# Moving the last batch's near scores and three batches' near values from the projection into the second attention

## The chip, the cores and the metric

One core of one Trainium2 chip runs the whole program. The metric is the device time in microseconds of one execution, from three timed runs, and one further execution that was profiled. All times inside the program are taken from that profiled execution and count from the start of its span.

## What is computed

The program is a two-layer language-model tower over 8 sequences (batches) of 512 rows of 256 numbers. Layer 0 is an embedding, a causal attention and a feed-forward block. Layer 1 is the part that matters here. Its attention gives each of 16 heads a window of its own, and scales each head by a gate:

```
windows = [max(4, 256 // 2**h) for h in range(16)]
q, k = split(x @ Wqk + bqk);  v = k
mask = (j <= i) & (j > i - windows[h])
att  = softmax(where(mask, q @ k.T / 4, -inf))
gated = (att @ v) * softmax(x @ Wgate + bgate)[..., None]
out  = gated @ Wproj + bproj
```

Heads 0 to 5 have windows from 256 down to 8 keys; the other ten heads have a window of 4 keys. After it comes a mixture-of-experts block with 8 experts, two for each row, and one shared expert.

## The kernel before

The program is a row of blocks. Inside a block each engine has its own instruction list and waits on semaphores; at the end of a block all engines meet, and the next block begins on all of them together. `project_local` and `attend` are two such blocks, one right after the other, and the change is about them.

**The projection, `project_local`.** It runs over the 8 batches. For each batch TensorE makes queries and keys, VectorE (DVE) adds the bias and writes them to `qkr` (L831), and the six wide heads are turned and split into three bf16 terms: ScalarE (ACT) makes the first and the second (L740, L752), GpSimd (POOL) the third (L789, in `third_term`). SyncE (SP) stores those terms in device memory with six transfers for a batch, three for queries (L643, `q_dram`) and three for keys (L644, `k_dram`), 96 partitions each.

The ten near heads, with 4 keys for each row, are not done on TensorE. SP stores the batch's keys (L627), loads them back shifted by 0, 1, 2 and 3 rows into `near` (L636, a ring of three buffers), and then DVE multiplies keys with queries (L836), sums over 16 elements (L841), adds the mask of the first rows (L846), takes the maximum (L849), subtracts it (L851), waits for ACT's exponential (L744), and makes the shares (L856, L858, L861, L865), which it leaves in `near_shares` (called `pw`, a ring of two). POOL then multiplies shares with keys into `near_values` (called `pv`, L795), adds halves (L800) and adds again into `attn` (L802): this is `near_values(b)`.

DVE's loop has nine turns. Turn n makes the rows of batch n and the near scores of batch n-1, so the ninth turn holds only the near scores of the last batch. POOL's loop for batch b waits (except for the last) until the near product of batch b is done, makes the third term of b, and then does `near_values(b-1)` for b from 1 to 6. The near values of batches 6 and 7 are left to the next block.

**The attention, `attend`.** It handles the six wide heads in 16 units of three heads (two units for each batch). SP loads the unit's terms. TensorE makes scores into a ring of two slots, `psA`; DVE reduces each slot to a row maximum (L1334), and TensorE may fill a slot again only when DVE has reduced it. The maxima are turned, sent to device memory and read back (L1177, L1179) into two further rows of the queries, and a second set of products gives scores from which ACT takes exponentials (L1304). Values and sums come from TensorE (L1262), and DVE divides, multiplies by the gate (L1353) and writes `attn` (L1356). The whole is a software pipeline, four units deep. POOL begins with four memsets (L1128), does `near_values` of batches 6 and 7 (L1118, L1123, L1125), and adds the output bias to the residual (L1134).

Nothing here is planned by costs: the order on each engine is the order of the text.

Of the kernel before, what the change touches and what calls it, by code (L numbers as in the profile page):

```python
# [17 lines left out]
P = 128  # L18
F32 = mybir.dt.float32
# [558 lines left out]
def project_local(nc, res, ident, rstd, shift, w_qk, b_qk, w_g, b_g, q_dram, k_dram, v_dram, k_rows, gates, attn,  # L578
                  near, pv, pw, b_out, bias_out):

# [3 lines left out]
    with ExitStack() as ctx:  # L584
# [10 lines left out]
        zero = k.sb("zero", [B, NW * DW])  # L595
        edge = k.sb("edge", [P, NW])
        prod = k.sb("prod", [P, NW, TG, DW])
# [8 lines left out]
        names = ("raw hi wt tab pad ones edged xn xT xTh xTl q qs vs rows gt gl gexp gdone R h rest m l "  # L606
                 "prod sc0 sc1 sc2 sexp sg sdone pv1 pv2 pv3").split()
        s = {n: k.sem(n) for n in names}
# [6 lines left out]
        def _(sp):  # L615
# [23 lines left out]
            def terms(b):  # L639
                par = b % 2  # L640
                sp.wait_ge(s["l"], b + 1)
                for term in range(NTERM):
                    sp.dma_start(q_dram[b, :, DK * term:DK * (term + 1), :], part[0:PW, par, term, 0, :]).then_inc(s_out[par], 16)  # L643
                    sp.dma_start(k_dram[b, :, DK * (2 - term):DK * (3 - term), :], part[0:PW, par, term, 1, :]).then_inc(s_out[par], 16)  # L644

            for b in range(B):
                rows(b)
                if b >= 1:
                    terms(b - 1)
            terms(B - 1)  # L650
            for n in range(2):
                sp.wait_ge(s_out[n], 16 * NL * (B // 2))
                sp.wait_ge(s_vout[n], 16 * (B // 2))
# [57 lines left out]
        def _(act):  # L711
# [49 lines left out]
            for b in range(B):  # L761
# [8 lines left out]
                if b + 2 < B:  # L770
                    normed(b + 2)
            near_exp(B - 1)

        @block.gpsimd
        def _(pool):
# [15 lines left out]
            def near_values(b):  # L791
                pool.wait_ge(s["sdone"], 3 * b + 3)
                if b >= 1:
                    pool.wait_ge(s["pv3"], b)
                pool.tensor_tensor(pv[:].rearrange("p n t (h d) -> p (n t h) d", d=DK),  # L795
                                   near[:, b % 3].rearrange("p n t (h d) -> p (n t h) d", d=DK),
                                   pw[:, b % 2].rearrange("p n t h -> p (n t h)").unsqueeze(2).to_broadcast([P, NW * TG * DH, DK]),
                                   ALU.mult).then_inc(s["pv1"], 1)
# [11 lines left out]
            pool.wait_ge(s["pv3"], B - 2)  # L810
            pool.wait_ge(s["l"], B)

        @block.vector
        def _(dve):
# [39 lines left out]
            def near_shares(b):  # L854
# [7 lines left out]
                dve.wait_ge(s["sg"], b + 1)  # L862
                if b >= 2:
                    dve.wait_ge(s["pv1"], b - 1)
                dve.tensor_tensor(pw[:, b % 2], sc, ssum[:].unsqueeze(1).to_broadcast([P, NW, TG, DH]), ALU.mult  # L865
                                  ).then_inc(s["sdone"], 1)
# [29 lines left out]
            dve.wait_ge(s["edged"], 2)  # L896
            for n in range(B + 1):
                if n < B:
                    rows(n, (0, 1))
                if n >= 1:  # L900
                    near_products(n - 1)
                if n < B:
                    rows(n, (2, 3))
# [6 lines left out]
                if n < B:  # L910
                    gate_logits(n)
                    rests(n)
                if n >= 1:
                    near_shares(n - 1)
                if n < B:
                    gate_shares(n)
            dve.wait_ge(s["sdone"], 3 * B)

# [154 lines left out]

def attend(nc, tag, windows, bands, q_dram, k_dram, v_dram, m_dram, gates, near, pv, pw, ident, attn, res, bias):

# [14 lines left out]
    with ExitStack() as ctx:  # L1090
# [14 lines left out]
        s_load, s_values = ([k.sem(f"{name}{n}") for n in range(2)] for name in ("load", "values"))  # L1105
        names = "const scoresA max topT_ps topT m_out m_in scoresB exp pv outT turned rec norm near1 near2 near3 biased".split()
        s = {n: k.sem(n) for n in names}
# [6 lines left out]
        def _(pool):  # L1114
            def near_values(n, b):
                if n:
                    pool.wait_ge(s["near3"], n)
                pool.tensor_tensor(pv[:].rearrange("p n t (h d) -> p (n t h) d", d=DK),  # L1118
                                   near[:, b % 3].rearrange("p n t (h d) -> p (n t h) d", d=DK),
                                   pw[:, b % 2].rearrange("p n t h -> p (n t h)").unsqueeze(2).to_broadcast([P, NW * TG * DH, DK]),  # L1120
                                   ALU.mult).then_inc(s["near1"], 1)
# [7 lines left out]
            pool.wait_ge(s["const"], 4)  # L1129
            for n in range(2):  # L1130
                near_values(n, B - 2 + n)
# [4 lines left out]
            pool.wait_ge(s["near3"], 2)  # L1136

# [149 lines left out]
        def _(act):  # L1287
            def stage(u):
                for what, n in events(windows, u):
# [24 lines left out]
        def _(dve):  # L1314
            def stage(u):
                for what, n in events(windows, u):
# [27 lines left out]
                    elif what == "OUT":  # L1344
# [6 lines left out]
                        if windows is not None:  # L1351
# [1667 lines left out]
def tower(nc, a):  # L3019
    Kit.used.clear()  # L3020
    with ExitStack() as ctx:
# [16 lines left out]
        with ExitStack() as ctx1:  # L3038
# [11 lines left out]
            with nc.sbuf_tensor("attn1", [P, NT, D], F32) as attn, nc.sbuf_tensor("gates", [P, NT, H], F32) as gates, \  # L3050
                    nc.sbuf_tensor("bias_out", [P, D], F32) as bias_out:
                with nc.sbuf_tensor("near", [P, 3, NW, TG, DW], F32) as near, \
                        nc.sbuf_tensor("near_values", [P, NW, TG, DW], F32) as pv, \
                        nc.sbuf_tensor("near_shares", [P, 2, NW, TG, DH], F32) as pw:
                    project_local(nc, res, ident, rstd1, shift1, a["w_qk1"], a["bqk"], a["w_g1"], a["bgate"], q1_dram, k1_dram, v1_dram,
                                  k_rows, gates, attn, near, pv, pw, a["bproj"], bias_out)
                    attend(nc, "att1", windows, bands, q1_dram, k1_dram, v1_dram, m_dram, gates, near, pv, pw, ident, attn,
                           res, bias_out)
# [59 lines left out]
```

## Time and profile before

| | us |
|---|---|
| median of 3 timed runs | 1414.05 |
| lowest, highest | 1412.55, 1414.31 |
| profiled execution, whole | 1406.67 |
| its span | 1404.9 |
| PE (TensorE) busy in the span | 1228.1 |
| DVE busy | 838.8 |
| POOL busy | 682.2 |
| ACT busy | 646.5 |

The span is the profiled execution without what lies around it (1.77 us). The projection runs from some 517 us to 655.70 us, the second attention from there to some 793 us. Busy shares of the whole say little about these two stages; the rows below are read from the boundary between them.

### The profile page before, as it was taken

The page shows a single profiled execution, that of the slowest core. Times are in us where ns is not written, and L with a number is a line of the kernel's source. Part 1 is how long each engine was busy: PE and PEld are TensorE (multiplying, and loading weights), DVE is VectorE, ACT ScalarE, POOL GpSimd, SP SyncE. Part 2 cuts the span into 40 slices and gives each one's busy share as a digit, 9 for nine tenths or more (in the row PEclk, how much of TensorE's full clock was granted, in tenths as well). Part 3 has the DMA queues.
Part 4 walks back from the last instruction along what each step waited for, and adds up shares of the span by engine and source line. Part 5 has one row for each costly group of instructions (what it writes and reads, how often), then busy time and mean ns, then how long its engine had stood idle before and what let it go on. Part 6 is the DMA issues. An engine that isn't in the chain of part 4 may idle for free. (4 is left out here: it accounts for less than half of the span.)

```text
span 1404.9 us, 29240 instructions
## 1 busy us (share of the span) xinstructions
PE 1228.1 (87%) x9665; PEld 961.1 (68%) x9666; DVE 838.8 (60%) x1784; ACT 646.5 (46%) x1249; POOL 682.2 (49%) x621
## 2 busy tenths in 40 slices
PE   5886999999978949892899785989989999999996
PEld 3664555555546837771666674989977888888885
DVE  4998788888837957995655394633333333333332
ACT  2882566666665544440344463222323334333332
POOL 6856687777352220877800000366224555555453
PEclk9996899999999977775899998999999999999999
DMA  2497999999500004665354321000347335465331
GB/s 56 141 280 230 273 278 280 276 288 292 130 3 2 1 28 133 190 185 153 93 115 97 105 80 41 16 26 28 108 162 216 54 52 141 114 166 139 52 56 21
DMA packets 123608, 179.16 MB, mean 128 GB/s; under 512 B 26953, under 2 KB 84592, under 8 KB 123512
## 3 DMA queue, kind: packets, MB, share of 16 engines
q1 hardware_dynamic: 106808, 159.62, 39.2%
q0 software_dynamic: 16704, 18.31, 7.9%
q8 instruction: 54, 0.88, 0.3%
q14 instruction: 42, 0.34, 0.1%
HBM read 104.60 MB, written 74.18 MB: 127 GB/s over the span
## 5 line engine op out<-in xcount | busy, mean ns | idle before, releaser
L1637 DVE TENSOR_REDUCE att_top<-att_psS 128x4 f32<-128x512 f32 (+2 forms) x192 | 194.9, 1037 | 41.6 <-PE att_psS L1524 40.0
L2851 POOL DMA_INDIRECT out<-ffn1c_y,ffn_table x71 | 112.3, 1582 | 164.3 <-DMA out<-ffn1c_y,ffn_table 76.7
L2984 DVE TENSOR_TENSOR ffn1c_hid<-ffn1c_psG,ffn1c_sil 128x512 f32<-128x512 f32 x71 | 49.1, 692 | 135.7 <-PE ffn1c_psG L2889 135.7
L1608 ACT ACTIVATE att_prob<-att_psS 128x1024 f32<-128x1024 f32 (+1 forms) x96 | 83.3, 887 | 61.6 <-PE att_psS L1538 61.6
L1518 PE MATMUL att_psS<-pairs_ka,pairs_qa 48*128 48x384 f32 (+3 forms) x512 | 100.3, 401 | 9.8 <-DMA pairs_ka<-k_parts 5.3
L2889 PE MATMUL ffn1c_psG<-ffn_high,ffn1c_xh 128*128 x284 | 96.4, 421 | 4.8 <-DVE ffn1c_xl L2975 2.7
L1608 ACT ACTIVATE pairs_part<-att_psS 128x1024 f32<-128x1024 f32 (+1 forms) x96 | 83.0, 888 | 34.3 <-PE att_psS L1538 34.3
L2593 POOL DMA_INDIRECT ffn_rows<-normed_rows,ffn_table x71 | 70.0, 986 | 55.4 <-DVE ffn_gate L2467 25.4
L2444 POOL DMA_INDIRECT slots<-ffn1b_entry,ffn1b_sloti x64 | 64.1, 1002 | 61.1 <-DVE ffn1b_sloti L2532 23.8
L1538 PE MATMUL att_psS<-pairs_qa,pairs_ka 50*128 50x256 f32 (+3 forms) x512 | 88.8, 388 | 3.0 <-DVE att_top L1637 0.9
L2889 PE MATMUL ffn1c_psG<-ffn_high,ffn1c_xl 128*128 x284 | 89.9, 397 | 0.0
L2889 PE MATMUL ffn1c_psG<-ffn_low,ffn1c_xh 128*128 x284 | 89.6, 397 | 0.0
L2949 ACT CAST ffn1c_hh<-ffn1c_psH 128x512 fp32r<-128x512 f32 x71 | 41.7, 587 | 87.2 <-PE ffn1c_psH L2900 85.9
L1334 DVE TENSOR_REDUCE att_top<-att_psA 128x2 f32<-128x768 f32 (+3 forms) x64 | 51.3, 813 | 47.7 <-PE att_psA L1215 46.9
L1524 PE MATMUL att_psS<-m_later,m_half 64*128 64x128 bf16 x1024 | 77.9, 234 | 0.0
L2942 ACT ACTIVATE ffn1c_sil<-ffn1c_psG 128x512 f32<-128x512 f32 x71 | 42.5, 598 | 64.9 <-PE ffn1c_psG L2889 64.9
L2975 DVE TENSOR_TENSOR ffn1c_xl<-ffn1c_psX,ffn1c_xh 128x256 fp32r<-128x256 f32 x71 | 30.2, 425 | 69.9 <-ACT ffn1c_xh L2935 67.9
L1304 ACT ACTIVATE att_prob<-att_psB 128x384 f32<-128x384 f32 (+4 forms) x112 | 48.9, 472 | 49.0 <-PE att_psB L1229 48.5
L1518 PEld LDWEIGHTS att_psS<-pairs_ka,pairs_qa 48*128 48x128 f32 x512 | 53.3, 201 | 26.2 <-issue 14.6
L2699 ACT ACTIVATE ffn1b_sil<-ffn1b_psG 128x256 f32<-128x256 f32 x64 | 24.6, 385 | 101.0 <-PE ffn1b_psG L2660 79.5
L1538 PEld LDWEIGHTS att_psS<-pairs_qa,pairs_ka 50*128 50x128 f32 x512 | 43.6, 188 | 34.7 <-issue 23.1
L2957 ACT ACTIVATE ffn1c_y<-ffn1c_psY,ffn_gate 128x256 f32<-128x256 f32 x71 | 33.7, 474 | 68.4 <-PE ffn1c_psY L2914 61.6
(397 smaller groups left out, 3534.9 us busy)
## 6 DMA issues: line engine op xcount, KB each, us to landing
prep_raw<-in_w_all SPq DMA_DIRECT2D x27, 512.0 KB, 5.7
experts_hi<-ffn0w_room SPq DMA_DIRECT2D x27, 512.0 KB, 6.4
experts_lo<-prep_lo SPq DMA_DIRECT2D x27, 512.0 KB, 7.4
ffn_high<-experts_hi SPq DMA_DIRECT2D x24, 512.0 KB
ffn_low<-experts_lo SPq DMA_DIRECT2D x24, 512.0 KB
near<-near_keys SPq DMA_DIRECT2D x32, 320.0 KB
q_parts<-pairs_part SPq DMA_DIRECT2D x8, 1024.0 KB
k_parts<-pairs_part SPq DMA_DIRECT2D x16, 512.0 KB
```

Of the source, the lines that this page charges most:

```text
L1304: act.activation(dst, src, ACT.Exp, scale=0.25).then_inc(s["exp"], 1)
L1334: dve.tensor_reduce(dst, src, AX.X, ALU.max).then_inc(s["max"], 1)
L1518: pe.matmul(psS[:, bank, g, col:col + cols], qa[r, u % LOADED, q, P * i:P * (i + 1)], ka[r, u % LOADED, q, 0:cols], start=True, stop=True, ...
L1524: mm = pe.matmul(psS[:, bank, g, col + cols - P:col + cols], half[r, part, :], later[r, part, :], start=False, stop=True, tile_position=(6 ...
L1538: mm = pe.matmul(psS[:, bank, g, col:col + cols], ka[r, v % LOADED, q, P * j:P * (j + 1)], qa[r, v % LOADED, q, P * j:S], start=True, stop ...
L1608: act.activation(dst, src, ACT.Exp, scale=0.25).then_inc(s["exp"], 1)
L1637: dve.tensor_reduce(dst, src, AX.X, ALU.max).then_inc(s["max"], 1)
L2444: pool.indirect_dma_start(out=self.dram["table"], in_=self.entry[:, t, n, :], in_offset=None, out_offset=bass.IndirectOffsetOnAxis(ap=self ...
L2593: pool.indirect_dma_start(out=rows[:, t % 4, :], out_offset=None, in_=dram["rows"], in_offset=bass.IndirectOffsetOnAxis(ap=table[:, t:t + ...
L2851: pool.indirect_dma_start(out=rows_out, in_=y[:, t.buf, :], in_offset=None, out_offset=bass.IndirectOffsetOnAxis(ap=table[:, t.value:t.val ...
L2889: mm = pe.matmul(psG[:, t.par, g, :], x[:, t.par, P * c:P * (c + 1)], w[:, bass.ds(at, 1), col:col + F1], start=(q == 0), stop=(q == 5))
L2984: dve.tensor_tensor(hid[:, t.par, :], psG[:, t.par, 1, :], sil[:, t.par, :], ALU.mult).then_inc(s["act"], 1)
```

## The change

DVE's loop now has eight turns, so that the last batch's near scores leave the projection. A new class `Late` holds what they need in SBUF: the last batch's near queries (copied there by POOL at the end of the projection), the mask of the first rows, the scores, maximum, sums and shares. `attend` begins on DVE with `late_shares`, the nine instructions of those scores, ahead of the first maximum of unit 0; ACT does their exponential ahead of its walk. `near_values` of three batches (5, 6, 7) now run on POOL in `attend`; the first must wait until DVE has read the products out of `pv`, which both use. `near_shares` has three buffers instead of two. In the projection, POOL makes the third term of batches 6 and 7 without waiting for a near product. The last batch's three stores of keys' terms are issued by ACT's queue, the three of queries still by SP's. SP waits for the last `near` loads before the block ends.

```
 project_local, SP, terms(b):
-        sp.dma_start(k_dram[b, ...], part[0:PW, par, term, 1, :]).then_inc(s_out[par], 16)
+        if b < B - 1:
+            sp.dma_start(k_dram[b, ...], part[0:PW, par, term, 1, :]).then_inc(s_out[par], 16)
+ at its end: sp.wait_ge(s_near[(B - 1) % 3], 16 * NW * ((B - 1) // 3 + 1))
 project_local, ACT, after the loop:
-        near_exp(B - 1)
+        act.wait_ge(s["l"], B)
+        for term in range(NTERM):
+            act.dma_start(k_dram[B - 1, :, DK * (2 - term):DK * (3 - term), :], part[0:PW, (B - 1) % 2, term, 1, :])
 project_local, POOL:
         for b in range(B):
-            if b < B - 1:
+            if b < B - 2:
                 pool.wait_ge(s["prod"], b + 1)
             third_term(b)
-            if 1 <= b < B - 1:
+            if 1 <= b < B - 2:
                 near_values(b - 1)
+        pool.wait_ge(s["qs"], TG * B)
+        pool.tensor_copy(late.q_rows[:], qkr[:, (B - 1) % 2, :, PW:D]).then_inc(s["kept"], 1)
 project_local, DVE:
-        for n in range(B + 1):        # near scores of n - 1 in every turn n >= 1
+        for n in range(B):
 attend, POOL:
     def near_values(n, b):
+        pool.wait_ge(s["late"], 9 if b == B - 1 else 2)
-    for n in range(2): near_values(n, B - 2 + n)
+    for n in range(3): near_values(n, B - 3 + n)
 attend, ACT:
+        act.wait_ge(s["late"], 5)
+        act.activation(late.scores[:], late.scores[:], ACT.Exp, scale=0.25).then_inc(s["late_exp"], 1)
         walk(act, stage, groups)
 attend, DVE:
+        def late_shares():            # each waits for the one before it, the sums also for ACT
+            pv = near[:, b % 3] * late.q_rows           # 128x2560, late = 1
+            sc = reduce add over 16 of pv               # 128x160, late = 2
+            sc[:, :, 0, :] += late.edge                 # 128x40
+            late.largest = reduce max of sc             # 128x40
+            sc -= late.largest                          # 128x160, late = 5
+            late.sums = reduce add of sc                # after late_exp
+            late.shares = reciprocal of late.sums
+            late.shares *= gates of the last batch      # 128x40
+            pw[:, b % 3] = sc * late.shares             # 128x160, late = 9
+        late_shares()
         walk(dve, stage, groups)
```

The lines inside `late_shares` are written short here. All its operands are in SBUF; in the projection the scores were in PSUM.

## Rows read from the trace of the kernel before

**Rows 1.** Windows of the second attention: us, busy by engine, clock, DMA share, GB/s.
```profile
core 0: us, PE busy (x) PEld busy (x) DVE busy (x) ACT busy (x) POOL busy (x), PEclk, DMA share, GB/s
663.00:671.00 8.00, 6.92 (x54) 5.15 (x52) 5.82 (x10) 0.00 (x0) 7.76 (x4) 0.67 0.62 110
703.00:711.00 8.00, 7.33 (x91) 5.42 (x88) 4.90 (x11) 3.88 (x9) 0.00 (x0) 1.00 0.48 104
```

**Rows 2.** Timeline, PE and DVE as the attention starts: start, duration, instruction, idle before.
```profile
660.57 0.40 PE L1212 MATMUL att_psA<-bands_never,bands_idb 128*128 128x256 bf16 x1 [25.71 <-DMA att_ka<-k_parts]
...
662.76 0.50 PE L1213 MATMUL att_psA<-bands_mask_q,bands_idb 128*128 128x384 bf16 x1 [0.41 <-DVE att_top L1334]
...
661.75 1.42 DVE L1334 TENSOR_REDUCE att_top<-att_psA 128x2 f32<-128x768 f32 x2 [10.45 <-PE att_psA L1215]
```

**Rows 3.** Timeline of SP's queue at the end of the projection.
```profile
637.72 0.76 SPq L643 DMA_DIRECT2D q_parts<-qkv_part  x1
...
641.71 0.74 SPq L644 DMA_DIRECT2D k_parts<-qkv_part  x1
647.76 0.74 SPq L643 DMA_DIRECT2D q_parts<-qkv_part  x1
...
651.71 0.74 SPq L644 DMA_DIRECT2D k_parts<-qkv_part  x1
```

**Rows 4.** Waits of SP's queue, 600 to 700 us: total, times, longest.
```profile
SPq L652 <- DMA k_parts<-qkv_part: 2.4, 1, 2.4
```

**Rows 5.** Timeline of ACT: the last batch's second term.
```profile
638.50 1.05 ACT L752 CAST qkv_part<-qkv_rest 96x1024 bf16<-96x1024 f32 x1 [0.91 <-DVE qkv_rest L889]
```

**Rows 6.** Timeline of POOL, from the projection's end into the attention.
```profile
631.87 2.13 POOL L789 TENSOR_TENSOR qkv_part<-qkv_rest,qkv_part 96x1024 bf16<-96x1024 f32 x1 [2.76 <-DVE qkv_prod L836]
...
643.03 4.70 POOL L789 TENSOR_TENSOR qkv_part<-qkv_rest,qkv_part 96x1024 bf16<-96x1024 f32 x1
655.70 5.33 POOL L1128 MEMSET att_ka<- 2x1536 bf16 x4 [7.97 <-POOLq L584]
661.11 4.55 POOL L1118 TENSOR_TENSOR near_values<-near,near_shares 128x2560 f32<-128x2560 f32 x1
665.74 2.88 POOL L1123 TENSOR_TENSOR near_values<-near_values 128x1280 f32<-128x1280 f32 x1
668.70 1.54 POOL L1125 TENSOR_TENSOR attn<-near_values 128x640 f32<-128x640 f32 x1
```

**Rows 7.** Windows of one us at the two ends of term stores, columns as Rows 1.
```profile
643.00:644.00 1.00, 0.00 (x0) 0.00 (x0) 1.00 (x1) 0.00 (x0) 1.00 (x2) 0.50 0.41 144
645.00:646.00 1.00, 0.00 (x0) 0.00 (x0) 0.97 (x2) 0.00 (x0) 1.00 (x1) 0.50 0.23 80
654.00:655.00 1.00, 0.00 (x0) 0.00 (x0) 0.00 (x0) 0.00 (x0) 0.00 (x0) 0.50 0.12 42
```

**Rows 8.** Timeline of DVE: the last batch's near scores, first to last.
```profile
642.63 3.12 DVE L836 TENSOR_TENSOR qkv_prod<-near,qkv_qkr 128x2560 f32<-128x2560 f32 x1 [2.29 <-DMA near<-near_keys]
645.79 2.83 DVE L841 TENSOR_REDUCE qkv_psS<-qkv_prod 128x160 f32<-128x2560 f32 x1
648.65 0.21 DVE L846 TENSOR_TENSOR qkv_psS<-qkv_psS,qkv_edge 128x40 f32<-128x40 f32 x1
...
649.25 0.33 DVE L851 TENSOR_TENSOR qkv_psS<-qkv_psS,qkv_smax 128x160 f32<-128x160 f32 x1
...
650.75 0.20 DVE L861 TENSOR_TENSOR qkv_ssum<-qkv_psS,gates 128x40 f32<-128x40 f32 x1
650.98 0.32 DVE L865 TENSOR_TENSOR near_shares<-qkv_psS,qkv_ssum 128x160 f32<-128x160 f32 x1
```

**Rows 9.** Line L1353: count, then duration in ns, min/median/max, first and last start.
```profile
L1353 DVE TENSOR_TENSOR att_rec<-att_rec,gates x16: 170/172/1947, 687.5 to 792.3; 128x12 f32<-128x12 f32 x16
```

**Rows 10.** Timeline of DVE and of POOL: its slowest execution, and what POOL ran.
```profile
693.70 1.95 DVE L1353 TENSOR_TENSOR att_rec<-att_rec,gates 128x12 f32<-128x12 f32 x1 [0.28 <-DVE att_rec L1349]
...
679.40 18.53 POOL L1134 TENSOR_TENSOR m_res<-m_res,bias_out 128x1024 f32<-128x1024 f32 x8
```

**Rows 11.** Line L836: duration in ns, min/median/max.
```profile
L836 DVE TENSOR_TENSOR qkv_prod<-near,qkv_qkr x8: 2815/2830/3157, 544.8 to 642.6; 128x2560 f32<-128x2560 f32 x8
```

More of the change, by code:

```diff
@@ L578, in project_local @@
 def project_local(nc, res, ident, rstd, shift, w_qk, b_qk, w_g, b_g, q_dram, k_dram, v_dram, k_rows, gates, attn,
-                  near, pv, pw, b_out, bias_out):
+                  near, pv, pw, late, b_out, bias_out):
     with ExitStack() as ctx:
@@ L595, in project_local @@
         zero = k.sb("zero", [B, NW * DW])
-        edge = k.sb("edge", [P, NW])
+        edge = late.edge
         prod = k.sb("prod", [P, NW, TG, DW])
@@ L650, in _ @@
             terms(B - 1)
+            sp.wait_ge(s_near[(B - 1) % 3], 16 * NW * ((B - 1) // 3 + 1))
             for n in range(2):
@@ L771, in _ @@
                     normed(b + 2)
-            near_exp(B - 1)
+            act.wait_ge(s["l"], B)
+            for term in range(NTERM):
+                act.dma_start(k_dram[B - 1, :, DK * (2 - term):DK * (3 - term), :], part[0:PW, (B - 1) % 2, term, 1, :]
+                              ).then_inc(s_out[(B - 1) % 2], 16)
         @block.gpsimd
@@ L909, in _, with __init__ @@
                     near_scores(n - 1)
-                if n < B:
-                    gate_logits(n)
-                    rests(n)
+                gate_logits(n)
+                rests(n)
                 if n >= 1:
                     near_shares(n - 1)
-                if n < B:
-                    gate_shares(n)
-            dve.wait_ge(s["sdone"], 3 * B)
+                gate_shares(n)
+            dve.wait_ge(s["sdone"], 3 * (B - 1))
+            dve.wait_ge(s["gdone"], 3 * B)
+class Late:
+    def __init__(self, k):
+        self.q_rows = k.sb("q_rows", [P, TG, DW])
+        self.edge = k.sb("edge", [P, NW])
+        self.scores = k.sb("scores", [P, NW, TG, DH])
+        self.largest, self.sums, self.shares = (k.sb(n, [P, TG, DH]) for n in ("largest", "sums", "shares"))
 class Unit:
@@ L1071, in make, with attend @@
         pool.wait_ge(s_done, n + 4 * len(self.windows))
-def attend(nc, tag, windows, bands, q_dram, k_dram, v_dram, m_dram, gates, near, pv, pw, ident, attn, res, bias):
+def attend(nc, tag, windows, bands, q_dram, k_dram, v_dram, m_dram, gates, near, pv, pw, late, ident, attn, res, bias):
     groups, HG = (len(windows), len(windows[0])) if windows else (NHG, H // NHG)
@@ L1105, in attend @@
         s_load, s_values = ([k.sem(f"{name}{n}") for n in range(2)] for name in ("load", "values"))
-        names = "const scoresA max topT_ps topT m_out m_in scoresB exp pv outT turned rec norm near1 near2 near3 biased".split()
+        names = "const scoresA max topT_ps topT m_out m_in scoresB exp pv outT turned rec norm late late_exp near1 near2 near3 biased".split()
         s = {n: k.sem(n) for n in names}
@@ L1129, in _ @@
             pool.wait_ge(s["const"], 4)
-            for n in range(2):
-                near_values(n, B - 2 + n)
+            for n in range(3):
+                near_values(n, B - 3 + n)
             for b in range(B):
@@ L1314, in _ @@
         def _(dve):
+            def late_shares():
+                b, sc = B - 1, late.scores
+                dve.tensor_tensor(pv[:], near[:, b % 3], late.q_rows[:].unsqueeze(1).to_broadcast([P, NW, TG, DW]),
+                                  ALU.mult).then_inc(s["late"], 1)
+                dve.wait_ge(s["late"], 1)
+                dve.tensor_reduce(sc[:].rearrange("p n t h -> p (n t h)"),
+                                  pv[:].rearrange("p n t (h d) -> p (n t h) d", d=DK), AX.X, ALU.add).then_inc(s["late"], 1)
+                dve.wait_ge(s["late"], 2)
+                dve.tensor_tensor(sc[:, :, 0, :], sc[:, :, 0, :], late.edge[:].unsqueeze(2).to_broadcast([P, NW, DH]), ALU.add
+                                  ).then_inc(s["late"], 1)
+                dve.wait_ge(s["late"], 3)
+                dve.tensor_reduce(late.largest[:], sc[:].rearrange("p n t h -> p t h n"), AX.X, ALU.max).then_inc(s["late"], 1)
+                dve.wait_ge(s["late"], 4)
+                dve.tensor_tensor(sc[:], sc[:], late.largest[:].unsqueeze(1).to_broadcast([P, NW, TG, DH]), ALU.subtract
+                                  ).then_inc(s["late"], 1)
+                dve.wait_ge(s["late_exp"], 1)
+                dve.tensor_reduce(late.sums[:], sc[:].rearrange("p n t h -> p t h n"), AX.X, ALU.add).then_inc(s["late"], 1)
+                dve.wait_ge(s["late"], 6)
+                dve.reciprocal(late.shares[:], late.sums[:]).then_inc(s["late"], 1)
+                dve.wait_ge(s["late"], 7)
+                dve.tensor_tensor(late.shares[:], late.shares[:], gates[:, tiles_of(b), PH:H], ALU.mult).then_inc(s["late"], 1)
+                dve.wait_ge(s["late"], 8)
+                dve.tensor_tensor(pw[:, b % 3], sc[:], late.shares[:].unsqueeze(1).to_broadcast([P, NW, TG, DH]), ALU.mult
+                                  ).then_inc(s["late"], 1)
             def stage(u):
```

32 lines of the change are left out of this document (16 added, 16 removed).

## The prediction

> **What bounds the kernel now.** The change touches one place, the boundary at 655.70 us between the projection and the second attention, so I read the windows first, to see what the attention is bound by, and then the timelines of each engine around the boundary.
>
> In the attention's steady part TensorE is busy 7.33 of 8 us and DVE 4.90 [rows 1]. TensorE sets its pace, but only once the pipeline runs. At its start the two work in turns: TensorE fills two slots, and the third slot waits for DVE's first maximum (0.41 us of idle before the matmul at 662.76) [rows 2]. A microsecond lost at the start, by TensorE or by DVE, is a microsecond of the whole, since the stage after it begins only when the attention has ended.
>
> TensorE has nothing to do for 25.71 us before its first matmul of the attention at 660.57, and what ends this is a load of key terms [rows 2]. Followed back: the loads start with the block at 655.70, where POOL's first memset also starts [rows 6]; the block starts when SP has seen the last stored term land, a wait of 2.4 us [rows 4] after the sixth issue, which began at 651.71 and ended at 652.45 [rows 3]; the first of the six began at 647.76, when POOL's third term of the last batch was done (643.03 + 4.70 = 647.73) [rows 3, 6]. That instruction has two reasons to be late. ACT had its input ready at 639.55 (638.50 + 1.05) [rows 5], but POOL was in `near_values` until 643.03; and it then took 4.70 us where the one for the batch before took 2.13 [rows 6], because DVE's near product ran from 642.63 to 645.75 [rows 8]: 645.75 plus some 2 us is its end. DVE's own chain for the last batch ends at 651.30 [rows 8], 3.1 us before the last stored byte, so it does not set the end of the block.
>
> **The change part by part.** I call the start of the attention block T0; it is 655.70 now.
>
> *The third term.* The last batch's no longer queues behind `near_values(5)`, and DVE's near product of batch 7 is gone. It starts at 639.6 and, at 2.13 us, ends at 641.75: 6.0 us earlier than 647.73. That of batch 6 loses its wait, but DVE's product of batch 6 runs then and holds it to the same place, so I price it at nothing (631.87 + 2.13 still).
>
> *The stores.* SP is busy with batch 6's six stores until 642.45 (641.71 + 0.74) [rows 3]. Three more issues, at (651.71 - 647.76) / 5 = 0.79 us each, bring it to 644.8, and with the 2.4 us of landing [rows 4] and the 0.85 us from there to T0 (655.70 - 652.45 - 2.4) the block would start at 648.1, 7.6 us earlier. ACT's three issues run beside SP's, from 641.8 to 644.2, if they cost what SP's cost. But the data must also get through. Batch 6's stores are still being drained until 645.56: in that stretch the DMA share is 0.41 and the rate 144 GB/s, and it falls to 0.23 in the microsecond from 645 [rows 7]. The share never rises above this 0.41 while only term stores are in flight, though six were queued, so I take it as the rate at which these stores drain, from whichever queue they come. The last batch's six stores hold 6 x 98,304 bytes, which at 144 GB/s is 4.1 us after 645.56, so 649.65. Now the data end at 654.3 (share 0.12 of some 0.39 in the microsecond from 654) [rows 7]. So T0 moves by 4.65 us, to 651.05. The two ends are 4.65 (the stores of both queues share one drain) and 7.6 (only the issues count). I take 4.65, nearest to the measured drain.
>
> The Trainium skill has a rule on this (DMA: Bandwidth & Descriptors, "Issuing engines are not separate DMA queues"): transfers started by different engines run on the same 16 DMA engines, and starting them from several saves only the sequencer's time. By this rule the gain is the 4.65, and by a queue of its own for ACT the 7.6. The trace has no ACT store to compare.
>
> *POOL's copy of the queries* (128x640) lies after the third term and before 645; a 128x640 addition takes 1.54 us [rows 6], which is covered by the stores. SP's new wait for the near loads is over at 642.63 [rows 8]. Both cost nothing unless the stores end before 643.3.
>
> *DVE's nine instructions in the attention.* In the projection they took from 642.63 to 651.30, 8.67 us with ACT's exponential among them [rows 8]. Now they begin at T0. Without any stall DVE would be free at T0 + 8.7, while its first maximum now starts at T0 + 6.05 (661.75 - 655.70) [rows 2]. That alone costs 2.6 us, and it is the low end.
>
> But there is a stall. L1353 multiplies two small SBUF operands and takes 0.172 us in the median of 16 and 1.947 at most [rows 9]. The slow one started at 693.70 and ended at 695.65; POOL was then in a row of eight additions from 679.40, 2.316 us each, the seventh of which ended at 695.61 [rows 10]. So a DVE instruction with two SBUF inputs waits until the POOL instruction that was there first is over, and POOL waits the same way (the 4.70 us above). Of the nine, five have two SBUF inputs: the product, the mask, the subtraction, the gate, and the last. In the projection all but the product read their scores from PSUM.
>
> The Trainium skill says the same (SBUF — State Buffer, "Who interferes with whom"): the shared port pair is an exclusive lock, and a DVE instruction with two SBUF inputs contends with a GpSimd instruction that reads SBUF, not with one that only writes. By it the four memsets at the block's start do not hold up the product, nor it them; no row here shows that pair.
>
> Laid out from T0, each number with its row: product 2.83 (the median of L836) [rows 11], sum 2.83, to 5.7 with gaps. This releases POOL's first `near_values`; its memsets were over at 5.33 [rows 6]. The mask (0.21) starts first, since an instruction behind its own engine's semaphore begins some 0.04 us later and another engine's some 0.08 (645.79 after 645.75, and 631.87 after 631.79). Ends 5.93. POOL's product of 4.55 then runs to 10.48, and the subtraction waits for it: 10.81. POOL's addition of 2.88, queued meanwhile, runs to 13.69. The exponential, sum and reciprocal fall in this. The gate multiplication waits: 13.89. POOL's second addition of 1.54 runs to 15.43, and the last instruction waits for it: 15.76 [rows 6, 8]. The first maximum starts at T0 + 15.8 and not at T0 + 6.05: **9.75 us later**. TensorE has then filled two slots and waits with the third. If DVE's last instruction slips in ahead of POOL's second addition, it is 8.2.
>
> *The clock.* TensorE was granted 0.50 (1.2 GHz) while idle before the attention [rows 7], and 0.67 as a mean of the stretch 663 to 671, after which it runs at 1.00 [rows 1]. With a second idle stretch of some 10 us right after its first two slots, it is at the lower level again for work that now has some of the higher. I put 0.5 us on it, an estimate between 0 and 1.5.
>
> *POOL* has 8.97 us more (4.55 + 2.88 + 1.54) and starts later; its bias additions end near T0 + 52 of a stage of 137 us: hidden, and as many L1353 meet them as now.
>
> **The sum.** -4.65 + 9.75 + 0.5 = +5.6 us on the profiled execution's 1406.67, so 1412.3. The timed median stands 7.4 above that execution; the same addition to it gives 1414.05 + 5.6 = **1419.6 us**.
>
> **The rivals.**
>
> *A. No lock at the wrong moment (not slower).* If POOL's memsets wait for DVE's first product, they end at T0 + 2.83 + 5.33 = 8.16, and POOL's first product comes when DVE has only its last small instruction left. The place is the first 8 us of the attention, and it decides at whether the memsets end before DVE's sum does. Price 2.6 instead of 9.75 + 0.5, so -4.65 + 2.6 = -2.0: 1412.0. For it: POOL's L789 did wait for a DVE product. Against it: that one reads SBUF, a memset does not. With the stores at their other bound it would be -5.0, 1409.
>
> *B. ACT's queue drains beside SP's.* T0 moves by 7.6, and with the stall the sum is -7.6 + 10.25 = +2.65: 1416.7. For it: the trace shows one queue only. Against it: 0.41 of the DMA engines looks like a limit of the transfers' form.
>
> *C. POOL gets in first.* If POOL's product goes ahead of the mask, the mask ends at 10.5, the subtraction waits for POOL's 2.88 (13.7), the gate for its 1.54 (15.5), and the last for the next batch's 4.55: T0 + 20.3, a delay of 14.3, so +10.1: 1424.2. For it: both are released by the same event. Against it: the 0.04 us.
>
> **How the numbers follow.** Forecast 0.6, A 0.17, B 0.13, C 0.10. Only a difference above 0.2%, 2.8 us, can be told from none. Of the forecast's own 1416 to 1422 nearly all is slower by more than this (0.54); C adds 0.10 and B, which lies on the line, 0.05: slower 0.69. A is split between faster (0.09) and the same (0.08), B gives 0.07 and the forecast 0.05 to the same; 0.02 of the latter I move to faster for what I don't see: same 0.20, faster 0.11. The range takes in A's centre at its low end and C at its high end: 1411.5 to 1425.
>
> **What would show it.** The third term of the last batch starts at 639.6 and takes 2.1 us. The attention's loads start near 651. In the attention's first 16 us the subtraction, the gate multiplication and the last of `late_shares` show durations of 4.5, 2 and 1.8 us instead of 0.2 to 0.3, each ending with a POOL instruction, and TensorE idles some 10 us before its third slot, ended by L1334's successor. If those instructions are short, the forecast is wrong and A holds; if the loads start near 648, B does.

## The result, and the profile after

The changed kernel takes 1417.07 us in the median of 16 runs (1414.43 to 1423.14), beside 1413.68 of the kernel before (16 runs, 1402.65 to 1417.38). The ratio is 1.0041, with a 95% interval of 1.0023 to 1.0060: slower by 0.41%, or 5.8 us of 1413.68 (the two medians by themselves are 3.4 us apart, the two means 5.5). The forecast was 5.6 us slower, and 1419.6 us as a time.

The profiled execution of the changed kernel has a span of 1416.5 us, 11.6 more than the one before. Only 5.8 of these belong to the change. ACT's second term of the last batch, the last mark ahead of what the change moves, starts at 644.98 where it started at 638.50 [rows 5]. These 6.48 us are not the change's: SP's first issue of the projection comes 7.31 us later (524.95, 517.64 before), so they were lost ahead of it, in instructions that the change leaves alone, and 0.83 came back in the projection's first batches. Both are within the spread of the runs. The interval from the same mark of batch 6 to this one is 13.00 us, and 12.98 before. So the stretches below are counted from that mark, from the block's start T0 (where POOL's first memset starts), and to the end of DVE's last output of the attention (792.87 before, 805.17 after):

| | before | after | difference |
|---|---|---|---|
| from the mark to T0 | 17.20 | 13.58 | -3.62 |
| from T0 to DVE's first maximum | 6.05 | 15.09 | +9.04 |
| from T0 to the attention's end | 137.17 | 146.61 | +9.44 |
| from the mark to the attention's end | 154.37 | 160.19 | +5.82 |
| from there to the end of the span | 612.03 | 611.33 | -0.70 |

The start of the attention on DVE, with the columns of the timelines before: start, duration, instruction, idle before it. The first nine are the near scores that stood in the projection [rows 8].

```profile
658.60 2.83 DVE L1335 TENSOR_TENSOR near_values<-near,late_q_rows 128x2560 f32<-128x2560 f32 x1 [11.78 <-PEq L584]
661.46 2.82 DVE L1338 TENSOR_REDUCE late_scores<-near_values 128x160 f32<-128x2560 f32 x1
664.32 0.20 DVE L1341 TENSOR_TENSOR late_scores<-late_scores,late_edge 128x40 f32<-128x40 f32 x1
664.55 0.42 DVE L1344 TENSOR_REDUCE late_largest<-late_scores 128x40 f32<-128x160 f32 x1
665.01 4.15 DVE L1346 TENSOR_TENSOR late_scores<-late_scores,late_largest 128x160 f32<-128x160 f32 x1
669.56 0.43 DVE L1349 TENSOR_REDUCE late_sums<-late_scores 128x40 f32<-128x160 f32 x1 [0.40 <-ACT late_scores L1328]
670.02 0.40 DVE L1351 RECIPROCAL late_shares<-late_sums 128x40 f32<-128x40 f32 x1
670.46 1.54 DVE L1353 TENSOR_TENSOR late_shares<-late_shares,gates 128x40 f32<-128x40 f32 x1
672.03 1.70 DVE L1355 TENSOR_TENSOR near_shares<-late_scores,late_shares 128x160 f32<-128x160 f32 x1
673.65 1.41 DVE L1377 TENSOR_REDUCE att_top<-att_psA 128x2 f32<-128x768 f32 x2
```

POOL in the same stretch, and its third term of the last batch ahead of it [rows 6]:

```profile
646.11 2.12 POOL L794 TENSOR_TENSOR qkv_part<-qkv_rest,qkv_part 96x1024 bf16<-96x1024 f32 x1 [5.84 <-ACT qkv_part L754]
648.17 0.71 POOL L816 COPY late_q_rows<-qkv_qkr 128x640 f32<-128x640 f32 x1
658.56 5.33 POOL L1144 MEMSET att_ka<- 2x1536 bf16 x4 [9.68 <-POOLq L584]
664.43 4.55 POOL L1134 TENSOR_TENSOR near_values<-near,near_shares 128x2560 f32<-128x2560 f32 x1 [0.54 <-DVE late_scores L1338]
669.06 2.88 POOL L1139 TENSOR_TENSOR near_values<-near_values 128x1280 f32<-128x1280 f32 x1
672.02 1.53 POOL L1141 TENSOR_TENSOR attn<-near_values 128x640 f32<-128x640 f32 x1
```

Read the two together. All three DVE instructions that wait have two SBUF inputs. The subtraction (L1346, 0.33 us in the projection) starts at 665.01 and ends at 669.16; POOL's product ends at 668.98. The gate multiplication (0.20 before) ends at 672.00, POOL's addition at 671.94. The last (0.32 before) ends at 673.73, POOL's second addition at 673.55. The reductions between them run side by side with POOL unharmed, and so do the memsets and DVE's product: 5.33 and 2.83 us, both as long as alone. The Trainium skill's exception (SBUF — State Buffer, "Who interferes with whom": a GpSimd instruction that only writes SBUF does not contend) agrees with these two rows.

TensorE's third slot, by its timeline, waits for DVE; the idle time was 0.41 us [rows 2]:

```profile
663.53 0.40 PE L1228 MATMUL att_psA<-bands_never,bands_idb 128*128 128x256 bf16 x1 [22.47 <-DMA att_ka<-k_parts]
...
674.66 0.50 PE L1229 MATMUL att_psA<-bands_mask_q,bands_idb 128*128 128x384 bf16 x1 [9.34 <-DVE att_top L1377]
```

The stores, by the queues' timelines of ACT and SP and by windows of one us (columns as Rows 1):

```profile
648.25 2.94 ACTq L776 DMA_DIRECT2D k_parts<-qkv_part  x3
649.42 2.50 SPq L643 DMA_DIRECT2D q_parts<-qkv_part  x3
```

```profile
649.00:650.00 1.00, 0.00 (x0) 0.00 (x0) 0.00 (x0) 0.00 (x0) 0.00 (x0) 0.50 0.41 145
655.00:656.00 1.00, 0.00 (x0) 0.00 (x0) 0.00 (x0) 0.00 (x0) 0.00 (x0) 0.50 0.35 123
657.00:658.00 1.00, 0.00 (x0) 0.00 (x0) 0.00 (x0) 0.00 (x0) 0.00 (x0) 0.50 0.04 15
```

SP's last wait of the projection, 2.4 us before [rows 4], with what it waits for (us in total, times, longest):

```profile
SPq L654 <- DMA q_parts<-qkv_part: 6.1, 1, 6.1
```

The last issue is over at 651.92, and the data still flow until 657. What ends the block is the drain, as in the forecast, and not the issues.

### The profile page after: what moved, and what is told of

It reads as the page before. It is cut to its first block and busy times, and to the rows that moved or that the text cites. A ratio compares the mean times of both kernels' runs of the same rounds, so it can differ in the third digit from the quotient of the medians.

```text
span 1416.5 us, 29239 instructions
## 1 busy us (share of the span) xinstructions
PE 1230.6 (87%) x9665; PEld 963.9 (68%) x9666; DVE 845.2 (60%) x1784; ACT 646.8 (46%) x1249; POOL 682.7 (48%) x622
```

## The experiments

Each kernel was timed in turns with the kernel before; its ratio to it and the interval stand with it. Its trace is counted from the same mark. The whole of a run scatters by several us, so the stretches carry the verdicts, but they scatter too: where the attention's code is the same or nearly so, its stage differs by 0.5 us (136.92 to 137.45 in the five kernels without the nine in it), by 0.57 (138.95 and 139.52) and by 1.40 (146.61 and 145.21), and the stretch from the mark to T0 by up to 1.3. A difference below some 1.5 us between two single traces is therefore not read as an effect. The table sums up what follows (us).

| kernel | mark to T0 | T0 to first maximum | T0 to end | mark to end |
|---|---|---|---|---|
| before | 17.20 | 6.05 | 137.17 | 154.37 |
| changed | 13.58 | 15.09 | 146.61 | 160.19 |
| POOL waits for all nine | 12.66 | 8.54 | 138.95 | 151.61 |
| without the nine | 12.92 | 6.24 | 137.45 | 150.37 |
| changed, SP stores all | 12.13 | 15.09 | 145.21 | 157.34 |
| near values of 5 moved, ACT stores | 12.87 | 6.21 | 137.20 | 150.07 |
| before, ACT stores | 17.01 | 6.44 | 136.92 | 153.93 |
| near values of 5 moved, SP stores | 13.59 | 6.04 | 137.06 | 150.65 |
| changed, POOL's work in pieces | 12.88 | 11.03 | 141.88 | 154.76 |
| POOL waits, SP stores all | 11.80 | 8.54 | 139.52 | 151.32 |
| the nine spread | 13.06 | 6.38 | 141.28 | 154.34 |
| the nine spread, POOL in pieces | 12.90 | 6.50 | 136.85 | 149.75 |

### POOL waits for all nine

```
 attend, POOL, near_values:
-        pool.wait_ge(s["late"], 9 if b == B - 1 else 2)
+        pool.wait_ge(s["late"], 9)
```

> The changed kernel, but POOL starts the first near values of the attention only when all nine near-score instructions of DVE are done, so that no POOL instruction that reads SBUF runs beside them. Theory (lock): in the changed kernel the nine take 15.1 us because three of them wait out a POOL instruction; here they take 8.7 us, as in the projection before, no one of the small ones over 0.5 us, DVE's first maximum starts 8.7 us into the attention instead of 15.1, and the stage that took 146.6 us takes about 140. On the whole about 6.4 us less than the changed kernel, 1 us less than the kernel before. Rival (the nine are slow by themselves in SBUF, or are slowed by the key loads that run beside them): they take 15 us again and nothing moves.

The nine take 8.59 us (658.19 to 666.78), from its timeline of DVE:

```profile
664.60 0.32 DVE L1346 TENSOR_TENSOR late_scores<-late_scores,late_largest 128x160 f32<-128x160 f32 x1
...
666.22 0.20 DVE L1353 TENSOR_TENSOR late_shares<-late_shares,gates 128x40 f32<-128x40 f32 x1
666.45 0.33 DVE L1355 TENSOR_TENSOR near_shares<-late_scores,late_shares 128x160 f32<-128x160 f32 x1
666.69 1.42 DVE L1377 TENSOR_REDUCE att_top<-att_psA 128x2 f32<-128x768 f32 x2
```

The same instructions in the same place, with the same key loads beside them, are back at 0.32, 0.20 and 0.33. One changed constant gives back 7.66 us of the stage (146.61 to 138.95; the expectation was about 140). The ratio is 0.9964 (0.9932 to 0.9997). The lock is shown, the rival is out.

### Without the nine

```
 attend, DVE:    -        late_shares()
 attend, ACT:    -        act.wait_ge(s["late"], 5) and the exponential
 attend, POOL:   -        pool.wait_ge(s["late"], ...)
```

> The changed kernel without the last batch's near scores: the nine DVE instructions, ACT's exponential and POOL's waits for them are left out, so the last batch's near values are made from old shares. This shows the gain at the boundary alone. Theory: the attention stage is back at 137.2 us (before: 137.2, changed: 146.6) and its start stays where the changed kernel has it, 3.6 us earlier than before when counted from the last batch's second term; so about 9.4 us less than the changed kernel and 3.6 less than before. Rival (part of the longer stage comes from POOL's third near value or from the clock): the stage stays 1 us or more above 137.2.

The stage is back at 137.45, with POOL's third near value in it. So this third near value costs nothing that can be seen, and the nine and their stall are all but 0.3 of the 9.44 us. Ratio 0.9952 (0.9915 to 0.9989).

### All stores on SP

```
 project_local, SP:   -  if b < B - 1:      (the three key stores of every batch)
 project_local, ACT:  -  its three stores
```

> The changed kernel, but all six stores of the last batch's terms are issued by SP, none by ACT. Theory (the stores drain at some 143 GB/s whichever queue they come from): the attention starts within 0.5 us of where the changed kernel has it, 13.6 us after the start of the last batch's second term, and the time is unchanged. Rival (the issues set the end): three issues more on SP's queue at 0.79 us each make the start 2.4 us later.

T0 comes 1.45 us earlier than in the changed kernel, not 2.4 later. So the rival is out, but the expectation (within 0.5 us) missed too. SP's last issue ends at 652.46, and its wait behind it is 2.9 us, against 2.4 in the kernel before: the drain still ends the block, but by 0.5 us only, and the issues come close to it. Two windows of its trace, near the drain's start and at its end:

```profile
649.00:650.00 1.00, 0.00 (x0) 0.00 (x0) 0.00 (x0) 0.00 (x0) 0.00 (x0) 0.50 0.41 144
653.00:654.00 1.00, 0.00 (x0) 0.00 (x0) 0.00 (x0) 0.00 (x0) 0.00 (x0) 0.50 0.41 143
```

Issues from ACT save nothing here. The stage is 1.40 us shorter than in the changed kernel, with the same code and the same first maximum at 15.09; this is unexplained, and is scatter as far as is known. Ratio 1.0011 (0.9979 to 1.0043): the rest of the change's cost is still in it, and the timing by itself can't tell it from the kernel before.

### Only the near values of batch 5 moved

```
 project_local, POOL:
-            if b < B - 1:
+            if b < B - 2:
                 pool.wait_ge(s["prod"], b + 1)
             third_term(b)
-            if 1 <= b < B - 1:
+            if 1 <= b < B - 2:
                 near_values(b - 1)
 share buffers: 2 -> 3, as in the change; the last three key stores on ACT
 attend, POOL:
-    for n in range(2): near_values(n, B - 2 + n)
+    for n in range(3): near_values(n, B - 3 + n)
 near scores of the last batch: in the projection, as before
```

> The kernel before with only a part of the change: near values of batch 5 moved to the attention with three share buffers, third terms without their wait, ACT's three stores; the near scores of the last batch stay in the projection. Theory: the stores and DVE's near chain now end close together (DVE's chain ends 12.8 us after the start of the last batch's second term, the attention can start some 0.85 us behind it), so the attention starts 3.5 us earlier than before, and its stage stays at 137.2 us: 3.5 us less than before, 9 less than the changed kernel. Rival (the near scores had to leave the projection for the boundary to move): DVE's chain is stretched by POOL's earlier work or ends later, and the attention starts less than 1 us earlier than before.

The attention starts 12.87 us after the mark and its stage takes 137.20: 4.30 us less than before, where 3.5 were expected. DVE's near chain now ends the projection (its last row starts at 654.02, the block at 654.85), and it does so no later than the stores do in the changed kernel. The rival (less than 1 us earlier) is out: the near scores did not have to leave. Ratio 0.9957 (0.9923 to 0.9990), the lowest of the kernels that compute everything.

### ACT's stores alone

```
 before, with the last batch's three key stores on ACT, ahead of near_exp(B - 1)
```

> The kernel before with one part of the change alone: the last batch's three stores of keys' terms issued by ACT. Theory (one drain at 143 to 144 GB/s for both queues, and no more than that): here the six stores find the drain empty and SP's six issues (4.7 us) and the drain (4.1 us) are about equally long, so ACT's queue can save 0.6 us at most; the attention starts 16.6 to 17.2 us after the start of the last batch's second term (17.2 before). Second theory, from the run without ACT's stores, where the rate stayed at 143 GB/s to the end while with them it fell to 123: a second queue makes the drain itself slower, so that it saves nothing or costs, 17.2 or later. Rival (queues drain beside each other): the stores end after three issues, the start is 2.4 us earlier, 14.8.

17.01 against 17.20: nothing, and far from the rival's 14.8. The second theory's 17.2 or later did not come either. ACT's three issues took 3.24 us here, SP's 2.32, and ACT's exponential stood behind them until 655.56. Ratio 0.9976 (0.9946 to 1.0006).

### Near values of batch 5 moved, stores on SP

```
 the fourth experiment without ACT's stores
```

> The kernel before with near values of batch 5 moved to the attention, third terms without their wait, and three share buffers; the last batch's near scores stay in the projection and all stores stay on SP. If ACT's stores are worth nothing, the attention starts 12.1 to 12.9 us after the start of the last batch's second term (DVE's near chain, whose data is ready at the same time as before, ends at 12.4 to 12.8), its stage takes 137.2 us, and the sum of 149.3 to 150.1 is the shortest of all: about 4.5 us less than before. If ACT's stores are worth their 2.4 us of issues, the start comes at 14 or later.

13.59, above the range. Two things end close together here. DVE's near product waited for the near loads until 4.71 us after the mark (647.12) instead of 4.13 before and 3.99 in the kernel with ACT's stores, and DVE's chain behind it ended at 655.49, 0.51 before T0. But the stores were late as well: SP's last issue ended at 651.29 and its wait took 4.0 us, to 655.3, only 0.2 before DVE's chain. So the near loads and the stores both landed later than in the kernel with ACT's stores, where that wait was over at 653.4. Here ACT's stores seem to be worth 0.7 us, in the pair of the changed kernel and the one with SP alone they cost 1.45; both lie within the scatter. The stage is 137.06, the ratio 0.9969 (0.9940 to 0.9997).

### POOL's work in pieces

```
 attend, POOL, near_values:
-        pool.tensor_tensor(pv, near[:, b % 3], pw[:, b % 3], ALU.mult)        128x2560
+        for i in range(NW): pool.tensor_tensor(pv[:, i], near[:, b % 3, i], pw[:, b % 3, i], ALU.mult)
-        pool.tensor_tensor(pv[:, 0:2], pv[:, 0:2], pv[:, 2:4], ALU.add)       128x1280
+        for i in range(2): pool.tensor_tensor(pv[:, i], pv[:, i], pv[:, i + 2], ALU.add)
```

> The changed kernel, but in the attention POOL's near product is cut into four instructions of 640 elements in a partition and its first addition into two; all of them run at the same moment as in the changed kernel. Theory (lock, held for one POOL instruction): a DVE instruction with two SBUF inputs waits for the rest of the POOL instruction that holds the lock, so the stretches get shorter with the pieces: none of the three stretched instructions over 1.7 us (they were 4.15, 1.54 and 1.70), the nine take 10 to 12 us instead of 15.1, the first maximum starts 10 to 12 us into the attention, and the stage takes 141.5 to 143.5. Rival (bandwidth is shared, or the order of semaphores is at fault): the cut changes nothing, 15 us again.

DVE's timeline, the three that wait:

```profile
663.43 0.88 DVE L1348 TENSOR_TENSOR late_scores<-late_scores,late_largest 128x160 f32<-128x160 f32 x1
...
665.61 1.12 DVE L1355 TENSOR_TENSOR late_shares<-late_shares,gates 128x40 f32<-128x40 f32 x1
666.76 1.32 DVE L1357 TENSOR_TENSOR near_shares<-late_scores,late_shares 128x160 f32<-128x160 f32 x1
```

They were 4.15, 1.54 and 1.70. A POOL piece takes 1.28 us in the mean, and no wait is longer than about one piece. The stage takes 141.88. The nine take 11.06 us and the first maximum comes at 11.03, both as expected. POOL works for longer (four pieces 5.06 us instead of 4.55), and it costs nothing that can be seen, since POOL has room. Ratio 1.0009 (0.9980 to 1.0037).

### POOL waits, and SP stores all

```
 the first and the third experiment together
```

> Two edits tried before, together: POOL's near values wait for all nine near-score instructions, and SP issues all stores. Theory: the parts add up: the attention starts 12.1 us after the start of the last batch's second term, its first maximum comes 8.6 us later, its stage takes 139 us, together 151.1 us (before 154.4, changed 160.2): 3.2 us less than before, and 1 to 2 us behind the version that keeps the near scores in the projection. Rival (the earlier start with SP's stores was chance): the start is at 12.7 to 13.6 again.

11.80, 8.54 and 139.52, together 151.32 of 151.1 expected. Ratio 0.9978 (0.9951 to 1.0005).

This agreement hides a loss ahead of the mark. In all other kernels the mark comes 12.98 to 13.07 us behind the same mark of batch 6; here it comes 15.10 behind it. POOL's third term and DVE's near product of batch 6:

```profile
636.27 2.14 POOL L790 TENSOR_TENSOR qkv_part<-qkv_rest,qkv_part 96x1024 bf16<-96x1024 f32 x1
636.68 4.41 DVE L840 TENSOR_TENSOR qkv_prod<-near,qkv_qkr 128x2560 f32<-128x2560 f32 x1 [0.90 <-DMA near<-near_keys]
```

DVE had to wait for the near loads of batch 6 and could start 3.98 us behind that batch's mark, where it starts at 2.99 in the changed kernel. The third term no longer waits for the product, so POOL was first, and DVE's product took 4.41 us instead of 3.30: in the changed kernel's trace DVE starts first (634.97, POOL 635.55). Counted from batch 6's mark to the attention's end this kernel takes 166.42 us, only 0.9 less than the kernel before (167.35). This order comes in one of the ten traces that have the change's early third term.

### The nine spread over DVE's idle stretches

```
 attend, DVE, stage(u), in the first four stages only:
+                if first and u.n == 3:  sum, mask, maximum, subtraction
                 for what, n in events(windows, u):
+                    if first and (u.n, what) == (2, "TOP"):  product
+                    if first and (u.n, what) == (3, "OUT"):  sums, reciprocal, gates, shares
 attend, ACT: the exponential at (3, "TOP"); POOL waits for all nine; SP stores all
```

> The change kept, but with the nine near-score instructions moved off the start of the attention: the product stands before the second unit's turned maxima (DVE is idle there for 3.8 us in the kernel before), the sum, mask, maximum and subtraction before the fourth unit's first maximum (idle for 3.15 us), the rest before the first output; ACT's exponential stands in its fourth stage, POOL's near values wait for all nine, SP issues all stores. Theory (what cost the change its gain was the place of the nine, at the one point where TensorE waits for DVE, and the lock on top of it): DVE's first maximum is back at 6.1 us, no one of the nine is stretched, the attention stage takes 137.2 to 139.0 us, its start is 11.8 to 12.9 us after the start of the last batch's second term, together 149.0 to 151.9 (before 154.4, changed 160.2), about 4 us less than before. Rival (the nine cost their 8.7 us of DVE wherever they stand in the attention, since it works in turns with TensorE there): the stage takes 141 us or more.

A miss in the stage. The first maximum is at 6.38 and none of the nine is stretched, but the stage takes 141.28, the rival's number for a reason that neither side had. POOL's near values, released by the nine, now start at 686.44, and 0.03 us later the first of DVE's multiplications by the gates arrives (the line of [rows 9, 10]):

```profile
685.97 0.33 DVE L1357 TENSOR_TENSOR near_shares<-late_scores,late_shares 128x160 f32<-128x160 f32 x1
686.21 0.23 DVE L1401 RECIPROCAL att_rec<-att_psM 128x12 f32<-128x12 f32 x1
686.47 4.55 DVE L1405 TENSOR_TENSOR att_rec<-att_rec,gates 128x12 f32<-128x12 f32 x1
691.05 0.36 DVE L1408 TENSOR_TENSOR attn<-att_psM,att_rec 128x192 f32<-128x192 f32 x1
```

An instruction of 12 elements takes 4.55 us, and TensorE, by its own timeline, stands behind it:

```profile
691.56 0.27 PE L1283 MATMUL att_psM<-m_ident,att_top 128*12 128x128 f32 x1 [3.23 <-DVE attn L1408]
```

Ratio 1.0014 (0.9981 to 1.0046): moving the work off the bad place won as much as was lost by moving a long POOL instruction onto another.

### Spread, with POOL in pieces

```
 the spread kernel with the pieces of the seventh experiment
```

> The kernel with the nine instructions spread over DVE's idle stretches, with one edit: POOL's near product is cut into four instructions and its first addition into two, as tried before. In the spread kernel none of the nine was stretched, but the stage still took 141.3 us, because the first multiplication by the gates came 0.03 us after POOL's first near product and took 4.55 us, with TensorE idle for 3.2 us behind it. Theory (the lock, met by another instruction): here that multiplication takes 1.3 us at most, and the stage 137.7 to 139.2 us, 2 to 3.5 us less than in the spread kernel; its start is 12 to 13 us after the last batch's second term as there, together 150 to 152. Rival (the longer stage comes from DVE's own 8.7 us and from the later end of POOL's work, not from that one wait): the stage stays at 140.5 us or more.

```profile
685.29 0.23 DVE L1403 RECIPROCAL att_rec<-att_psM 128x12 f32<-128x12 f32 x1
685.55 1.28 DVE L1407 TENSOR_TENSOR att_rec<-att_rec,gates 128x12 f32<-128x12 f32 x1
```

4.55 became 1.28, and the stage 136.85, somewhat under the expectation (137.7 to 139.2): the 8.7 us of DVE's near scores are hidden as far as can be seen. The one wait, with what stood behind it, was thus worth 4.4 us. From mark to end it is 149.75 us, the shortest of all, by 0.3; counted from SP's first issue of the projection it is 269.97, and 269.30 in the version that only moves batch 5's near values, so the two are not ranked. Ratio 0.9978 (0.9954 to 1.0002), which does not tell it from the version that only moves batch 5's near values (0.9957); of the two, that one is the simpler, and its interval lies below 1.

## Why the prediction was right

The direction and the mechanism held: the stall of the nine behind POOL outweighs the earlier start. That the sum agrees so closely (+5.6 forecast, +5.82 by the two traces) is luck. The gain at the boundary was 1.03 us smaller than its term and the stall 0.71 smaller, and the two misses nearly cancel; besides, such stretches scatter by about 1 us from trace to trace. The time itself, forecast at 1419.6, was 1417.07. Step by step:

- **Third term.** Forecast: 1.1 us behind the mark, 2.13 long. Measured: 646.11, which is 1.13 behind 644.98, and 2.12. That of batch 6 took 4.71 us instead of 2.13, since it now starts while DVE's product runs, but ended at nearly the same place: 4.72 us ahead of the mark (635.55 + 4.71 = 640.26), 4.50 before. Priced at nothing, rightly for this trace. The sum took for granted that DVE's product is first; where POOL was first (POOL waits, and SP stores all), the mark came 2.1 us late, and 1.1 of them is the product's longer wait.
- **The stores.** Forecast: T0 4.65 us earlier, 12.55 us after the mark. Measured: 13.58 after it, 3.62 earlier. The mechanism (the drain ends the block, two queues are no faster than one) held: with stores of both queues under way the rate was 142 to 145 GB/s, as with SP alone. The size was off by 1.0: the rate held for five microseconds and then was 123 for three, so that the data ended near 657 and not at 656.1, which is the forecast's end of the data counted from this trace's mark. The drop is worth some 0.4 us (an estimate, 3 us times 21 of 144 GB/s); what made up the rest is open. Nor is the drop tied to ACT's queue as such: with ACT's stores the rate stayed at 141 GB/s or more nearly to the end in two kernels (without the nine; POOL's work in pieces). With the near scores out of the projection and SP alone storing, T0 came 12.13, 11.80, 13.06 and 12.90 us after the mark (mean 12.5); with ACT's three stores 13.58, 12.66, 12.92 and 12.88 (mean 13.0). The means lie closer than either group spreads. The 11.80 is the kernel whose mark came 2.1 us late; from batch 6's mark the two means are 26.03 and 26.01. Whether ACT's queue makes the drain slower is left open; a gain of the size of its three issues (2.4 us) is excluded.
- **The stall.** Forecast: first maximum 9.75 us later, or 8.2 if DVE's last instruction slips in. Measured: 9.04, with all three waits where they were laid out. The 0.7 us are in the sum's assumption that POOL's next instruction waits until DVE's is over: it started at 669.06, 0.08 behind POOL's own last and before DVE's subtraction ended at 669.16. Nor did DVE need its whole own time behind POOL: its three ends came 0.18, 0.06 and 0.18 us after POOL's, where the sum had 0.33, 0.20 and 0.33. DVE pays for the lock here, POOL nearly nothing.
- **The clock.** Forecast: 0.5. What is left of the stage beyond the first maximum is 9.44 - 9.04 = 0.40, and it was not tried by itself. In the 8 us from 674 TensorE was granted 0.62 in the mean, in the 8 us of the same work before 0.61, so little of the 0.40 can be the clock's. In the same kernel with SP alone storing, the same remainder is -1.00 (8.04 - 9.04), so a term of 0.5 can't be told from scatter: it is neither confirmed nor refuted.
- **Rival A** (the memsets wait for DVE's product) is refuted by the rows of POOL and DVE above; **rival B** (a drain for each queue) by the windows above, by the runs with and without ACT's stores, and by ACT's stores alone (17.01 us to T0, and not 14.8); **rival C** (POOL goes ahead of the mask) by the mask's 0.20 us: DVE was first, as the 0.04 against 0.08 us had said (0.04 and 0.15 in this trace).

What the prediction did not see is that the largest part of the change was not needed: with the near values of batch 5 out of the way, the projection ends within a few tenths of the same time whether or not the near scores stay in it.

## What to carry to other kernels

Ask of every small DVE instruction on the critical path that has both its inputs in SBUF which POOL instruction that reads SBUF can be in front of it: the price is what is left of that one, whatever the size of the small one (4.15 us for 160 elements, 4.55 for 12). A wait that keeps POOL back removed it here (stage 138.95 instead of 146.61), but it only moves POOL's instruction, which can then meet another (4.55 us in the spread kernel). Cutting POOL's instruction shortens each such wait wherever it falls (141.88), at 0.5 us of POOL for each product. Together with a better place for the nine it hid them (136.85). And work moved across a block's border must not land on the few microseconds in which the next stage fills its pipeline; look first whether the smaller part of the move already makes something else the last.

## What was not expected of the hardware

- A DVE multiplication of 12 elements a partition took 4.55 us behind a POOL product, against 0.17 in the median of 16.
- Between two POOL instructions that follow one another a waiting DVE instruction got in at each of three borders, and POOL's next one started only 0.08 us behind its own last.
- Three issues on ACT's queue took 2.94 to 3.57 us in six kernels, where SP's take 0.79 each when it issues alone; in the changed kernel the drain of the stores fell from 142 to 123 GB/s near its end.
